# Splitting the weight multiply of the one-hots between GpSimd and VectorE in the count stage of a graph network kernel

## The reference

```
summed = segment_sum(x[src], dst, num_segments=N_NODES)
mean = summed / maximum(deg, 1.0)[:, None]
h = x @ W_self + mean @ W_neigh + b                      # SAGE, twice
...
h = xi[dst] + xj[src] + b_pre                            # PNA, twice
mean, mean_sq = segment_sum(h, dst) / degc, segment_sum(h * h, dst) / degc
mx, mn = segment_max(h, dst, N), segment_min(h, dst, N)
```

## Time and profile before

| | |
|---|---|
| Median of 3 runs | 1872.82 us |
| Lowest, highest | 1872.35, 1880.16 us |
| Span of the profiled execution | 1871.3 us |
| VectorE busy, whole span | 1499.0 us (80%) |
| TensorE matmul busy | 1394.3 us (75%) |
| GpSimd busy | 830.5 us (44%) |
| ScalarE busy | 443.6 us (24%) |
| Count stage, blocks 1 to 24 | 112.82 to 400.88 us of the span |

### The profile page before, as it was taken

One profiled execution on the slowest core, in us unless ns is written; L12 is line 12 of the kernel. 1 busy time (PEld: TensorE's weight loads), 2 busy tenths in 40 slices (PEclk: granted clock), 3 DMA queues, 4 the chain that ended last, 5 costly groups with the idle time before them and its releaser, 6 DMA issues.

```text
span 1871.3 us, 31118 instructions
## 1 busy us (share of the span) xinstructions
PE 1394.3 (75%) x11444; PEld 1038.9 (56%) x11444; DVE 1499.0 (80%) x3642; ACT 443.6 (24%) x1002; POOL 830.5 (44%) x843
## 2 busy tenths in 40 slices
PE   0247777766996679999999952746999999995164
PEld 0146666666986446676666631333666666664032
DVE  7899999978615698999999854959989999996377
ACT  4346666651001301111111110130111111111011
POOL 3600000000600447667667774133766766777340
PEclk9968888888999789999999975968999999998586
DMA  5313333332650446677777652152776777765321
GB/s 125 115 71 134 131 138 140 140 140 69 203 175 18 138 145 218 226 257 254 235 227 259 219 167 96 31 185 89 253 235 237 238 234 236 253 222 186 123 72 28
DMA packets 116258, 311.74 MB, mean 167 GB/s; under 512 B 20784, under 2 KB 72452, under 8 KB 115758
## 3 DMA queue, kind: packets, MB, share of 16 engines
q1 hardware_dynamic: 64848, 146.57, 22.4%
q10 hardware_dynamic: 23470, 105.20, 15.8%
q0 software_dynamic: 27824, 58.54, 11.0%
HBM read 167.97 MB, written 142.32 MB: 166 GB/s over the span
## 4 chain that ended last, share of the span: by engine, by line
PE 44%; DVE 25%; DMA 12%; issue 6%; ACT 6%; POOL 4%; ACTq 2%; DVEq 0%; SPq 0%; POOLq 0%
PE ps L1105 21%; PE ps L1221 7%; DMA scanned<-table,rest_idx 4%; DMA counts<-A 4%; PE ps L1202 4%; DVE scanned L2124 4%; ACT A L747 3%; DVE accs L2089 3%; DVE accs L2071 3%; DVE scanned L2120 3%; PE ps L1233 3%; POOL scanned L1045 2%; PE ps L1316 2%; PE ps L1130 2%; DMA A<-counts 1%
## 5 line engine op out<-in xcount | busy, mean ns | idle before, releaser
L1045 POOL DMA_INDIRECT scanned<-table,rest_idx x700 | 700.6, 1001 | 486.7 <-DMA table<-Y 178.5
L1105 PE MATMUL ps<-big,A 125*128 125x128 bf16 (+1 forms) x7500 | 713.7, 252 | 37.4 <-ACT A L747 18.4
L1105 PEld LDWEIGHTS ps<-big,A 125*128 125x128 bf16 x7500 | 598.9, 101 | 146.9 <-ACT A L747 29.5
L2120 DVE SCALAR_TENSOR_TENSOR scanned<-scanned,rest_neg 128x128 f32<-128x128 f32 x700 | 242.2, 346 | 69.2 <-DMA scanned<-table,rest_idx 62.7
L1221 PE MATMUL ps<-S,big 126*128 126x500 bf16 (+1 forms) x1050 | 244.1, 371 | 60.6 <-DMA S<-picks 26.9
L2124 DVE SCALAR_TENSOR_TENSOR scanned<-scanned,rest_neg 128x128 f32<-128x128 f32 x700 | 242.1, 346 | 0.0
L2089 DVE TENSOR_TENSOR accs<-accs,ps 128x1000 f32<-128x1000 f32 (+1 forms) x154 | 166.2, 1079 | 42.7 <-PE ps L1233 42.5
L1221 PEld LDWEIGHTS ps<-S,big 126*128 126x128 bf16 x1050 | 95.1, 101 | 163.2 <-DVE accs L2089 43.4
L2071 DVE TENSOR_TENSOR accs<-accs,ps 128x1000 f32<-128x1000 f32 (+1 forms) x154 | 166.0, 1078 | 3.4 <-DVE big L1753 3.4
L1130 PE MATMUL ps<-scanned 128*128 128x150 bf16 x1050 | 113.1, 249 | 66.7 <-DVE scanned L1637 66.7
L1233 PE MATMUL ps<-S,lift 128*128 128x500 bf16 (+1 forms) x350 | 99.7, 365 | 84.6 <-DVE accs L2071 63.1
(11 more groups left out here) (378 smaller groups left out, 1437.3 us busy)
## 6 DMA issues: line engine op xcount, KB each, us to landing
rest_history<-scanned SPq DMA_DIRECT2D x100, 896.0 KB
A<-counts ACTq DMA_DIRECT2D x75, 800.0 KB
S<-picks SPq DMA_DIRECT2D x60, 640.0 KB, 7.2
picks<-S ACTq DMA_DIRECT2D x25, 800.0 KB, 3.3
counts<-A ACTq DMA_DIRECT2D x25, 800.0 KB, 3.3
scanned<-table,rest_idx POOLq DMA_INDIRECT x700
table<-Y SPq DMA_DIRECT2D x10, 320.0 KB, 2.5
S<-picks SPq DMA_DIRECT2D x10, 160.0 KB, 4.7
```

What stands on the lines that cost most here:

```text
L1045: nc.gpsimd.indirect_dma_start(out=rows[:, w, s, :], out_offset=None, in_=tables[1 + l], in_offset=bass.IndirectOffsetOnAxis(ap=rest_idx[: ...
L1105: m = nc.tensor.matmul(acc[:, bank, 0:width], A[0:NB, slot, a, :], XS[0:NB, a, c, 0:width], start=a == 0 and c == 0, stop=a == NT - 1 and ...
L2120: v.scalar_tensor_tensor(hist[:, w, s, 0:F], last[:, 0:F], col, rows[:, w, s, :], ALU.add, ALU.max).then_inc(main.scan_ops, 1)
```

## The change

GpSimd gets the product with the weights for the last two of the six tiles of every step, and VectorE's L1637 keeps the first four (`DVE_TILES = 4`). A new semaphore `weighed` counts GpSimd's products. TensorE waits for it ahead of each step's matmuls, besides `onehots`. VectorE waits for it ahead of L1628, so that GpSimd has read `plain_s` of two steps ago. To free semaphores, the five `aligned_in` semaphores of the gathers of records become two: one for the first gather, one for the other four together.

```diff
+DVE_TILES = 4
...
-        aligned_in = [sem(f"aligned_in{j}") for j in range(COLS)]
+        aligned_in = [sem("aligned_in0"), sem("aligned_in_rest")]
+        weighed = sem("weighed")
...
-                    in_offset=bass.IndirectOffsetOnAxis(ap=wstartI[:, j:j + 1], axis=0)).then_inc(aligned_in[j], 16)
+                    in_offset=bass.IndirectOffsetOnAxis(ap=wstartI[:, j:j + 1], axis=0)).then_inc(aligned_in[min(j, 1)], 16)
...
+            for n in range(NT * PIECES):
+                h = n % 2
+                pool.wait_ge(marked, n + 1)
+                nc.gpsimd.tensor_tensor(
+                    hot_s[:, h, :, DVE_TILES:PT], plain_s[:, h, :, DVE_TILES:PT],
+                    heavy[:, STEP * n:STEP * (n + 1)].rearrange("p j t -> p (j t)")[:, DVE_TILES:PT].unsqueeze(1)
+                    .to_broadcast([P, P, PT - DVE_TILES]), ALU.mult).then_inc(weighed, 1)
...
+            pe.sem_inc(weighed, 1)
...
-                pe.wait_ge(aligned_in[i], 16)
+                pe.wait_ge(aligned_in[min(i, 1)], 16 * (COLS - 1) if i else 16)
...
                     pe.wait_ge(onehots, b * (2 * PIECES) + (2 * j + 3))
+                    pe.wait_ge(weighed, b * PIECES + (j + 2))
...
                 dve.wait_ge(tallied, n + 1)
+                if n > 1:
+                    dve.wait_ge(weighed, n)
...
-                v.tensor_tensor(hot_s[:, h], plain_s[:, h],
-                                by_step(heavy, n).unsqueeze(1).to_broadcast([P, P, PT]), ALU.mult)\
-                    .then_inc(onehots, 1)
+                v.tensor_tensor(hot_s[:, h, :, 0:DVE_TILES], plain_s[:, h, :, 0:DVE_TILES],
+                                by_step(heavy, n)[:, 0:DVE_TILES].unsqueeze(1).to_broadcast([P, P, DVE_TILES]),
+                                ALU.mult).then_inc(onehots, 1)
```

## The result

The changed kernel takes 1917.8 us (median) beside 1875.4 us for the kernel before in the same runs: a ratio of 1.022 with a 95% interval of 1.0197 to 1.0243. It is slower, by some 42 us, about 2%. One of its four runs was disturbed (2129 us) and is left out of the ratio. The profiled execution's span is 1915.6 us, 44.3 above the 1871.3 of before.

The account below looks back on a forecast made before the run. The prediction took VectorE to bound the count stage, with the loop of stores just beside it. Its terms 52.6 + 8.2 + 7 = 67.8 us on the span of 1871.3 gave 1939.1, as median 1941 us; range 1878 to 1986.

Parts of the forecast that it names:

- The hold: Count-stage steps: GpSimd's product holds up VectorE by 0.55 us, making a step 1.89 us and blocks 1 to 24 +52.6 us.
- the small select: GpSimd's 128-element operation at 84.68 us, taken to lengthen the L1637 over it by 0.11 us; basis for pricing the hold.
- The rule for the whole instruction: Count stage: the skill's mutual exclusion for GpSimd's whole product, 0.67 us a step, 1962 us; grouped with longer products.
- Block 0: Start of the count stage: the first product waits behind gathers and mask, +6.1 us, five longer steps +2.1, together +8.2 us.
- TensorE's clock: Count stage: TensorE waits more and gets its lower clock; an overrun of 0.87 us every third block, +7 us.
- TensorE at 1.2 GHz for good: Rival, count stage: TensorE always at the lower clock, 15.7 us a block, 1970 us; chance 0.07.
- Starved or longer products: Rival, count stage: GpSimd enters only when VectorE stops, 1958 us, or its product holds 0.67 us, 1962 us; chance 0.14.
- VectorE's rate: Rival, VectorE's third operation: shortened to runs of four it loses its rate, 0.13 us more, 1986 us; chance 0.06.
- No hold: Rival, count stage: H under 0.24 us, blocks stay at 12.0 us, only block 0's +6.1 stays, 1879 us; chance 0.15.
- faster: Rival, count stage: the loop shrinks with VectorE, blocks come down towards 10.34 us, at best 1839 us; chance 0.05.
- the loop of stores: Count stage: slab stores wait on ScalarE and TensorE, whose pieces wait on earlier stores; claimed to hold blocks at 12 us.
- The point of H = 0.24 us: Count stage: H is the product's price for VectorE per step; at 0.24 us a block stays at 12.00 us.

Follow-up runs that it names:

- one tile: The change with one tile of six to GpSimd instead of two (`DVE_TILES = 5`): 2196.6 us, ratio 1.0147 to the kernel before.
- other memory: Against the kernel before: VectorE multiplies all six tiles, GpSimd does the same-shaped product on spare buffers nobody else touches; 1935.0 us, ratio 1.0287.
- one input: Like other memory, but GpSimd copies 256 elements (one input) instead of multiplying two; a single run, 1920.6 us.
- PSUM version: The change with block 0 by VectorE alone and, in blocks 1 to 24, counting constants in PSUM; ratios to the kernel before 0.9947 and 0.9948.
- three tiles: The change with three tiles of six to GpSimd (`DVE_TILES = 3`); a single run, 2255.7 us, 4.1% above the kernel before.

## Why the prediction was right

The direction, the mechanism and its place were as forecast, and the range held the time. The predicted 1941 us is 23 too high. The hold accounts for that figure by itself, but only because three other misses cancel.

**The hold.** *"0.11 x 2 x 2 = 0.44, and 0.11 for handing over, 0.55 us."* Measured: 0.41 us, with the data anywhere, 0.21 with half the reads. The part worked out from the small select was right within 0.03; for the 0.11 us of handing over no run shows anything. A step is 1.75 us instead of 1.89, 0.14 x 168 = 23.5 us less. That this equals the gap between the forecast 67.8 and the measured 44.3 is luck: the rest of the stage came out 6 us above the forecast (see the clock), block 0 cost 6.6 us instead of 8.2, and the part behind the stage was 4.4 us shorter, where nothing was forecast. The 0.13 us saved by the shorter operation came out exactly (0.55 to 0.42).

**The rule for the whole instruction.** The Trainium skill's rule (SBUF — State Buffer, "Who interferes with whom") agrees with the traces in which instructions it names: VectorE with two SBUF inputs against a GpSimd operation that reads SBUF, nothing for a GpSimd write, a one-input reduction or a PSUM input. What the prediction made of it, the product's whole length added to each step (0.67 us, 1962 us), did not come: the product takes 0.61 us alone and costs VectorE 0.41. That does not refute exclusion to the product's end, since in four of the five runs with a full hold the missing 0.2 us can be the two starts that run under the other engine's work; only the run with one tile speaks for a shorter hold. The select of the earlier trace rows fits both accounts too: it ends at 84.97, and the L1637 over it at 85.38, 0.41 us later, its 0.55 less 0.14. So to scale its 0.11 us by the reads was one of two ways that agree here.

In the other direction GpSimd's product took 0.32 us longer behind VectorE's second operation in nearly every step. That cost VectorE no time by itself. The row that the prediction gave for this direction is another case: L1893 is a TENSOR_SCALAR, with one tensor as input, and the select beside it still took 0.65 us. So "two inputs in SBUF" is not the whole condition under which the two engines meet; no run here tests that operation.

**Block 0.** *"+6.1 us"* and 2.1 for longer steps. Measured: 5.6 for the third step (86.18 for 80.56), 0.64 of which is there because block 0 as a whole began later in this profile (78.22 for 77.58), and 5 x 0.28 = 1.4 us for the others. The stage began 6.57 us later, and undoing it gave 6.0 us back.

**TensorE's clock.** *"+7 us"*, called an estimate. The granted clock fell as said, from 0.89 to 0.77. VectorE's own sum for the stage is 24 x (7 x 1.75 + 0.96) = 317.0 us and the stage took 330.25, so 13.2 us lie above it, not 7; 2 to 3 of them stand ahead of the last L1604. Both factors of the estimate were off, in opposite directions. *"A step at the lower level is 2.76 us"* adds two durations whose records overlap; from step to step it is 2.35 us, so an overrun over 1.75 is 0.60 us and not 0.87. And it came in nearly every block instead of every third: at a granted clock of 0.75 or less 17 of the 23 full blocks took 13.7 to 13.95 us, and the six at 0.87 took 13.35 to 13.54, against 13.21 for VectorE alone. The effect grows as VectorE's step shortens: from the first to the last L1604, 166 steps, the time above VectorE's own sum is some 4 us with a step of 1.88 (other memory), 13 with 1.75, 18 with 1.71 (one tile) and 24 with 1.68 (one input). It swallows most of what a smaller hold would have given: steps of 1.68, 1.71 and 1.75 us all end at 13.55 to 13.61 us a block. I had treated it as an addition to the sum, where over these three it works as a floor; at a step of 1.43 us, in the PSUM version, the blocks are at 12.2 and the clock at 0.86.

**TensorE at 1.2 GHz for good** did not happen: both levels occur in the blocks. Its price was too high for the same reason; with 0.75 and 1.60 us from start to start it would be 7 x 0.75 + 5 x 1.60 = 13.25 us a block, hardly more than VectorE's own sum, so the time alone could not have told it apart. The granted clock does.

**Starved or longer products** did not happen in the form priced; GpSimd's product ran after every second operation of a step. **VectorE's rate** held for runs of four and, as the runs with one and three tiles show, would not have held for odd runs.

**No hold** and **faster** rest on the statement that the loop of stores holds a block at 12 us by itself. The 12.33 us of the prediction are from a stretch with a granted clock of 0.86; in blocks with the full clock the same loop turned in 11.2 us, and in 11.0 in the PSUM version. The blocks of that version were 12.2 us on average all the same, so the best case was no gain in them. The point of H = 0.24 us, worked out against 12.00, was not tested: no run had a step of 1.58 us, and the steps of 1.68 us already gave 13.55 us a block and not 12.7, so the point where the change turns into a loss most likely lies lower.

## What to carry to other kernels

An engine that stands idle is no free help when its reads shut out the busy one: price the work given away by the time that the giver is shut out (here 0.41 us for a product of 256 elements, two reads each) against the time saved (0.13 us for the same 256). Look in the trace for the one place where the two already overlap; a single operation of 0.66 us among 174 of 0.55 carried this forecast. Where several limits lie within some per cent of each other, as VectorE, the store and TensorE's clock did, an experiment on one of them shows little until another is moved too, and an average over blocks hides which one it was: look at the blocks one by one.

## What I had not expected

- A 16-bit comparison in which one input comes from PSUM runs as fast as from SBUF (610 and 616 ns for 900 elements) and stays out of GpSimd's way. That turned the loss into a version that works.
- A VectorE product over runs of five or three bf16 values takes 0.58 us for 640 and for 384 elements; over runs of four it takes 0.42 us for 512, and in one run 0.55 us for 768.
- GpSimd's product takes 0.61 us for 256 outputs and 0.62 us for 128 with every sixth element read.
- Three kernels with different VectorE steps (1.68, 1.71, 1.75 us) were equally long in the stage within 0.5%, most blocks of each at a granted clock of 0.75.
